# A state-space stage whose next batch's inputs are made between the scan's steps

## The reference, cut to what matters

```python
x = einsum('ed,bld->bel', in_proj_w, hidden_states)          # 256 -> 512 channels
u = silu(conv(x, conv_w, 4 taps) + conv_b)
dt_lo, Bm, Cm = split(einsum('ke,bel->bkl', x_proj_w, u))    # 16 + 16 + 16 rows
delta = softplus(dt_proj_w @ dt_lo + dt_proj_b)
state = state * exp(delta_t * A) + (delta_t * u_t) * B_t      # over the 512 positions
y_t = sum over states of state * C_t
y = (y + D * u) * silu(z)          # z: the normalized x; y is added to x
```

## Time and profile before

| | us |
|---|---|
| median of 3 runs (3116.88 to 3126.09) | 3119.8 |
| the profiled execution | 3117.0 |
| its span, first to last instruction | 3115.6 |
| VectorE busy over the span | 2025.2 (65%) |
| TensorE busy over the span | 2485.5 (80%) |

### The profile page before, as it was taken

How to read it: one execution, slowest core, us unless ns; L and a number is a source line. 1 busy time by engine, 2 the same in 40 slices (tenths; PEclk the granted TensorE clock), 3 DMA queues, 4 the chain that set the end, 5 groups by cost and what they waited for, 6 DMA issues and landing times. The chain is left out here.

```text
span 3115.6 us, 42764 instructions
## 1 busy us (share of the span) xinstructions
PE 2485.5 (80%) x11156; PEld 1737.0 (56%) x11174; DVE 2025.2 (65%) x3184; ACT 1250.8 (40%) x2245; POOL 1586.5 (51%) x1294
## 2 busy tenths in 40 slices
PE   7825655555979489999999983889989999999686
PEld 2301212214767367667777762677777777877443
DVE  3579999897868334554444446675776676565596
ACT  3424343443345232221121212545545545555365
POOL 2446565564047666666666626654664655444110
PEclk9869899898989799999999996999999999999899
DMA  2016666653369798887777745443443543342101
GB/s 84 9 41 214 219 210 223 219 202 118 141 238 339 264 316 287 306 277 247 247 235 255 248 148 180 145 139 126 146 140 105 166 139 115 95 136 82 54 0 54
DMA packets 260696, 538.30 MB, mean 173 GB/s; under 512 B 24401, under 2 KB 90065, under 8 KB 259809
## 3 DMA queue, kind: packets, MB, share of 16 engines
q1 hardware_dynamic: 207296, 347.98, 32.9%
q0 software_dynamic: 44032, 167.80, 16.3%
q10 hardware_dynamic: 9248, 21.11, 2.0%
HBM read 328.14 MB, written 208.67 MB: 172 GB/s over the span
## 5 line engine op out<-in xcount | busy, mean ns | idle before, releaser
L523 PE MATMUL ps_y<-c_state,ident 128*128 128x512 f32 x512 | 268.7, 651 | 205.5 <-DVE c_state L475 205.4
L448 POOL TENSOR_TENSOR b_u<-du,bc 128x1024 f32<-128x1024 f32 x128 | 301.3, 2354 | 214.5 <-DVE c_state L475 178.0
L1713 ACT ACTIVATE prob<-ps_s,neg,q_rs 128x512 f32<-128x512 f32 x256 | 197.1, 774 | 330.5 <-DVE neg L1893 330.5
L1230 PE MATMUL ps_o<-w_dn,hid_t 96*128 x632 | 308.4, 611 | 0.0
L1797 POOL TENSOR_SCALAR prob<-prob,rden 128x512 f32<-128x512 f32 x256 | 175.6, 696 | 253.9 <-DVE rden L1901 253.9
L523 PEld LDWEIGHTS ps_y<-c_state,ident 128*128 128x128 f32 x512 | 91.8, 198 | 381.8 <-DVE c_state L475 312.7
L467 DVE TENSOR_TENSOR_SCAN state<-ps_decay,b_u 128x1024 f32<-128x1024 f32 x128 | 293.1, 2290 | 16.1 <-issue 8.7
L1266 ACT ACTIVATE silu_g<-ps_gu 128x192 f32<-128x192 f32 x159 | 52.6, 331 | 546.5 <-PE ps_gu L1211 543.0
L419 ACT ACTIVATE ps_decay<-delta,a_neg 128x511 f32 x256 | 165.9, 681 | 225.5 <-DVE state L467 225.1
L1211 PE MATMUL ps_gu<-w_gu_high,rows_t_high 128*128 (+1 forms) x636 | 230.7, 363 | 11.0 <-POOL w_gu_low L1095 9.5
L1095 POOL TENSOR_TENSOR w_gu_low<-raw_gu,w_gu_high 128x1536 fp32r<-128x1536 f32 x64 | 222.4, 3475 | 12.0 <-POOL w_gu_high L1093 12.0
(11 more groups left out here) (317 smaller groups left out, 6071.5 us busy)
## 6 DMA issues: line engine op xcount, KB each, us to landing
rows_dram<-zeros SPq DMA_DIRECT2D x15, 3584.0 KB, 14.3
raw_gu<-in_gate_up POOLq DMA_DIRECT2D x64, 768.0 KB, 5.4
rows<-rows_dram SPq DMA_DIRECT2D x160, 256.0 KB, 3.9
y_dram<-y SPq DMA_DIRECT2D x158, 256.0 KB, 3.5
bc<-bc_dram SPq DMA_DIRECT2D x64, 512.0 KB, 5.8
w_q<-wq_dram SPq DMA_DIRECT2D x64, 512.0 KB, 3.7
w_o<-wo_dram SPq DMA_DIRECT2D x16, 2048.0 KB, 8.5
w_dn<-in_down POOLq DMA_DIRECT2D x64, 384.0 KB, 5.9
```

Of the source, the lines that this page charges most:

```text
L448: pool.tensor_tensor(out=b_u[:, ec % 2, :, :], in0=m.du[:, ds1(b * EC + ec), :].broadcast_to([P, G, SEQ]), in1=bc[:, par, 0, :, :], op=ALU ...
L523: mm = pe.matmul(ps_y[ec][:, :], c.ident[:, :], c_state[:, ec % 2, g, :], start=False, stop=False)
L1230: mm = pe.matmul(ps_o[par][:, :], hid_t[par][:, k, :], w_dn[:, ds1(slot), k, :].rearrange("p a f -> p (a f)"), start=k == 0, stop=k == 1)
L1713: act.activation(prob[:, qt, :], ps_s[qt % 2][:, :], ACT.Exp, scale=q_rs[:, k % 2, qt:qt + 1], bias=neg[:, qt:qt + 1], accum_out=den[:, qt ...
```

## The change

`ssm_inputs`, the first `norm_statistics` and `ssm_scan` become one function, `state_space`, without loops on the chip: all 128 steps are written out. Batch 0's inputs are made first, as before, with the statistics of the norm between. The inputs of batch b + 1 are made during the 32 steps of batch b: each engine, after its part of step q, runs `also(b, s)` with s = q % 32, which holds pieces of that work. The softplus becomes max(v, 0) + m + (log(1 + m) - ((1 + m) - 1)): `parts` makes Abs and Relu on ScalarE, `dens` and `rests` are one VectorE operation each for a block, and `both`, `sum_delta` and `delta_u` are one GpSimd operation each.

The steps of a batch now go through pairs of blocks: 16 steps over blocks 0 and 1, then 16 over blocks 2 and 3. Two banks hold the sums instead of four, and two others serve the inputs and the transposes. One load of B and C serves two steps, from a ring of three. Gates and additions to X are done block by block in `also`. The zero fills are spread over the 64 groups of two steps, some 4.6 tiles each.

```diff
-def ssm_inputs(nc, c, m, d):
+def state_space(nc, c, m, d):
...
+        STEPS = EC * NG
+        PAIR = 2 * NG
+        GROUPS = BATCH * STEPS // 2
+        BR = 3
...
+        def block_of(q):
+            b, s = q // STEPS, q % STEPS
+            return b, s, b * EC + s // PAIR * 2 + s % 2
...
+            def load_bc(g):
+                b, ng = g // (STEPS // 2), g % NG
+                wait(sp, product_made, 2 * (g - BR + 1))
+                for n in range(2):
+                    src = m.bc_dram[b:b + 1, n * DS + ng * G:n * DS + (ng + 1) * G, :]\
+                        .rearrange("a n l -> a (n l)").broadcast_to([P, G * SEQ])
+                    sp.dma_start(bc[:, g % BR, n, :, :].rearrange("p g l -> p (g l)"), src).then_inc(bc_loaded[g % BR], 16)
...
+            for g in range(GROUPS):
+                b, r = g // (STEPS // 2), g % (STEPS // 2)
+                if r == 0:
+                    sp.wait_ge(dbc_stored, (b + 1) * 16)
+                load_bc(g)
...
+                if r == 12 and b + 1 < BATCH:
+                    store_bc(b + 1)
+                for dram, skip, n in ((m.rows_dram, 0, FILLS * FILL), (m.y_dram, MINT, FILLS * FILL_Y)):
+                    first, last = g * n // GROUPS, (g + 1) * n // GROUPS
+                    if last > first:
+                        fill(dram, skip + first, skip + last)
+                        fills += 1
+            sp.wait_ge(filled, 16 * fills)
...
+            def convolve(ec, out):
+                for k in range(TAPS):
+                    mm = pe.matmul(out[:, :], conv_diag[:, ec * TAPS + k, :], x_pad[:, ec, k:k + SEQ],
+                                   start=k == 0, stop=k == TAPS - 1)
+                mm.then_inc(conv_done, 1)
...
+            def also(b, s):
...
+                if more and 4 <= s < 8:
+                    ec = s - 4
+                    if ec < 2 and b:
+                        pe.wait_ge(x_added, n - 1 + ec)
+                    if ec < 2 and not b:
+                        pe.wait_ge(pos_made, EC)
+                    if ec >= 2:
+                        pe.wait_ge(x_copied, nn + ec - 1)
+                    project(nb, ec, bank[ec % 2])
+                if more and s in (8, 9):
+                    ec = s - 8
+                    pe.wait_ge(x_copied, nn + 3 + ec)
+                    convolve(ec, bank[ec])
+                if more and s in (11, 12):
+                    ec = s - 9
+                    pe.wait_ge(u_made, nn + ec - 1)
+                    convolve(ec, bank[ec - 2])
+                if more and s == 14:
+                    project_u(nb, bank[0])
+                if more and s == 15:
+                    project_dt(nb, 0, bank[1])
+                if more and s == 16:
+                    project_dt(nb, 1, bank[0])
+                if s == 18:
+                    pe.wait_ge(*((pos_made, nn + 1) if more else (x_added, n)))
+                    turn(n, bank[1])
+                if s == 19:
+                    pe.wait_ge(*((pos_made, nn + 2) if more else (x_added, n - 1)))
+                    turn(n + 1, bank[0])
+                if more and s in (20, 21):
+                    pe.wait_ge(x_added, n + s - 19)
+                    project_dt(nb, s - 18, bank[(s - 19) % 2])
             pe.wait_ge(small_loaded, 128)
...
+            for q in range(BATCH * STEPS):
+                b, s, n = block_of(q)
+                e, r = s % 2, s % PAIR
+                if r == e:
+                    if n < 2:
...
+                        pe.wait_ge(y_gated, n - 1)
+                    pe.matmul(ps_y[e][:, :], d_diag[:, n % EC, :], slot(u, n), start=True, stop=False)
+                pe.wait_ge(product_made, q + 1)
+                for g in range(G):
+                    mm = pe.matmul(ps_y[e][:, :], c.ident[:, :], c_state[:, q % 2, g, :], start=False, stop=False)
+                mm.then_inc(product_used, 1)
+                if r >= PAIR - 2:
+                    pe.matmul(ps_y[e][:, 0:2], c.ident[:, :], zero2[:, :], start=False, stop=True).then_inc(y_summed, 1)
+                also(b, s)
...
+            def keep_x(b, ec, out):
+                act.wait_ge(x_made, b * EC + ec + 1)
+                wait(act, delta_made, (b - 1) * EC + ec + 1)
+                act.activation(x_pad[:, ec, TAPS - 1:], out[:, :], ACT.Copy).then_inc(x_copied, 1)
...
+            def parts(b, ec, out):
+                n = b * EC + ec
...
+                act.activation(mag[:, ec, :], out[:, :], ACT.Abs, bias=dt_b[:, ec:ec + 1]).then_inc(mag_made, 1)
+                act.activation(pos[:, ec, :], out[:, :], ACT.Relu, bias=dt_b[:, ec:ec + 1]).then_inc(pos_made, 1)
...
+            def decays(q):
+                b, s, n = block_of(q)
+                act.wait_ge(delta_made, n + 1)
+                wait(act, scanned, q - 1)
...
+            def also(b, s):
+                nb = b + 1
+                if s == 2:
+                    gates(b, (0, 1))
+                if s == 4:
...
+                    return
+                if 5 <= s < 9:
+                    keep_x(nb, s - 5, bank[(s - 5) % 2])
+                if s == 10:
+                    keep_u(nb, 0, bank[0])
+                    keep_u(nb, 1, bank[1])
+                if s == 13:
+                    keep_u(nb, 2, bank[0])
+                    keep_u(nb, 3, bank[1])
+                if s == 15:
+                    keep_dbc(nb, bank[0])
+                if s == 16:
+                    parts(nb, 0, bank[1])
+                if s == 17:
+                    parts(nb, 1, bank[0])
+                if s == 18:
+                    exponents(nb, (0, 1))
+                if s == 19:
+                    logarithms(nb, (0, 1))
+                if s == 21:
+                    parts(nb, 2, bank[1])
+                if s == 22:
+                    parts(nb, 3, bank[0])
+                if s == 23:
+                    exponents(nb, (2, 3))
+                if s == 24:
+                    logarithms(nb, (2, 3))
...
+            for q in range(BATCH * STEPS):
+                decays(q)
+                also(q // STEPS, q % STEPS)
...
+            def sum_delta(b, ec):
+                n = b * EC + ec
+                waits(both_made, n + 1)
+                waits(rest_made, n + 1)
+                waits(scanned, (b - 1) * STEPS)
+                pool.tensor_tensor(out=slot(delta, n), in0=pos[:, ec, :], in1=log_part(ec), op=ALU.add).then_inc(delta_made, 1)
...
+            def input_product(q):
+                b, s, n = block_of(q)
+                g = group_of(q)
+                waits(bc_loaded[g % BR], g // BR * 32 + 32)
+                waits(du_made, n + 1)
+                waits(scanned, q - 1)
+                waits(product_made, q - 2)
...
+            def also(b, s):
+                if b + 1 == BATCH:
+                    return
+                if s in (20, 21, 26, 27):
+                    both(b + 1, (20, 21, 26, 27).index(s))
+                if s in (22, 24, 28, 30):
+                    sum_delta(b + 1, (22, 24, 28, 30).index(s))
+                if s in (23, 25, 29, 31):
+                    delta_u(b + 1, (23, 25, 29, 31).index(s))
...
+            for q in range(BATCH * STEPS):
+                input_product(q)
+                also(q // STEPS, q % STEPS)
...
+            def rests(b, ecs):
+                for ec in ecs:
+                    n = b * EC + ec
+                    dve.wait_ge(den_made, n + 1)
+                    dve.wait_ge(log_made, n + 1)
+                    dve.tensor_tensor(out=log_part(ec), in0=log_part(ec), in1=den[:, ec, :], op=ALU.subtract)\
+                        .then_inc(rest_made, 1)
...
+            def apply_gate(n):
+                dve.wait_ge(y_summed, n + 1)
...
+            def also(b, s):
+                n = b * EC
+                if b and s == 0:
+                    apply_gate(n - 1)
+                if b and s == 3:
+                    add(n - 2, bank[0])
+                if b and s == 4:
+                    add(n - 1, bank[1])
+                if s == PAIR - 1:
+                    apply_gate(n)
+                if s == PAIR:
+                    apply_gate(n + 1)
+                if s == 19:
+                    add(n, bank[1])
+                if s == 20:
+                    add(n + 1, bank[0])
+                if s == STEPS - 1:
+                    apply_gate(n + 2)
+                if b + 1 == BATCH:
+                    return
+                if s == 19:
+                    dens(b + 1, (0, 1))
+                if s == 21:
+                    rests(b + 1, (0, 1))
+                if s == 24:
+                    dens(b + 1, (2, 3))
+                if s == 26:
+                    rests(b + 1, (2, 3))
...
+            dens(0, range(EC))
...
+            rests(0, range(EC))
+            scan(0)
+            for q in range(BATCH * STEPS):
+                if q + 1 < BATCH * STEPS:
+                    scan(q + 1)
+                product(q)
+                also(q // STEPS, q % STEPS)
+            last = BATCH * EC
```

(120 more changed lines are left out.)

402 lines of the change are left out of this document (134 added, 268 removed).

## The result

| | us |
|---|---|
| before, median of 4 | 3119.6 |
| after, median of 4 (3236.6 to 3262.2) | 3248.7 |
| ratio, 95% interval | 1.041 (1.036 to 1.046) |
| profiled execution of after, and its span | 3262.2, 3260.8 |

The kernel is slower by 129 us; 3271 was forecast, with a range of 3180 to 3336.

The account below looks back on a forecast made before the run. It took each 3.61 us step as bound by GpSimd's b_u and VectorE's product not running together. Terms 78.4 + 458.5 + 213 + 61 + 62 + 4 + 5.6 = 882.5, against 731.5, gave +151: 3271 us, range 3180 to 3336.

Parts of the forecast that it names:

- The mechanism: In eleven steps a batch ScalarE waits for TensorE, loses its lead, and the step becomes one chain.
- The start: Only batch 0's inputs come ahead of the scan, so the first product ends at 78.4 us.
- The waits and the clock: Three batches with pieces: chained steps add 213 us, TensorE at half clock behind gaps adds 61.
- plain steps: Scan steps without added waits: 3.61 us each, 127 after the first product, 458.5 us.
- the clock's share: TensorE passes behind gaps of waiting steps run at half clock: 61 us, bounds 0 and 124.
- Pieces of GpSimd and VectorE: Input pieces moved into the scan's steps: 62 us for three batches, 4 in the last; bounds 10 to 90.
- the pairs of `dens`: VectorE's differences within a batch's steps, put at 0.5 us.
- `rests` at s = 21: They feed GpSimd's sum_delta, holding b_u(23): about 4.3 us beside TensorE's chain, leaving GpSimd 1.2 behind.
- The tail: After the last product: sums, gate, transposes and two additions, 5.6 us.
- Late loads: Doubled loads of B and C during the scan, costed at nothing; bounds 0 and 32.3 us.
- The stages behind: Stages after the last addition to X, taken to be the same as before.
- u's steps: Waiting steps s = 10 and 13: 13.8 us each, 10.2 over a plain step, without the page's extra drain.

Follow-up runs that it names:

- e1: Changed kernel with ScalarE's pieces of the next batch's inputs three steps later: 3014.2 us, 0.965 of the kernel before.
- e3: Changed kernel plus six matmuls on zeros after each TensorE piece that ScalarE waits for, keeping TensorE at work: 3197.0 us, 1.026 of the kernel before.
- e2: Changed kernel with ScalarE's pieces one step later: 3074.6 us, 0.985 of the kernel before.
- e7: On top of e4, ScalarE's pieces two steps later than in the changed kernel, those of u three: 2989.6 us, 0.959 of the kernel before.
- e5: Changed kernel with ScalarE's pieces two steps later: 3017.1 us, 0.966 of the kernel before.
- e4: On top of e1, `dens` and `rests` made one a step and GpSimd's other pieces moved: 2992.5 us, 0.960 of the kernel before.
- e8: On top of e1, only the differences (`dens`) made one a step, GpSimd's pieces unmoved: 3005.5 us, 0.961 of the kernel before.
- e6: Changed kernel with TensorE's thirteen input pieces placed ahead of the sums of their step: 3095.5 us, 0.991 of the kernel before.

## Why the prediction was right

The mechanism, the sign and the place were right: see e1 and e3. By its terms, from the product ends in the profile after:

- **The start**: 75.5 for 78.4.
- **The waits and the clock**: 33 steps of 9.0 to 16.9 are 386.6 us, 267.5 over plain steps, for 213 + 61 = 274. With e3's clock the same steps are 344.8, so 225.6 over, for 213; the clock's share that e3 took away is 42, for 61.
- **Pieces of GpSimd and VectorE**: 846.5 - 75.5 - 458.5 - 267.5 = 45.0, for 66 (62 and the last batch's 4). This is the term that was mis-sized. A GpSimd piece costs 0.9 (steps of 4.5), not 1.52: while the product holds GpSimd off, the piece is already issued, and its wait and start fall in that time (the piece at 255.98 lasts 2.24 instead of 1.27, as the product ends at 257.10). Against it, the pairs of `dens` were put at 0.5, and the steps behind them are 3.6 over a plain one, 0.9 of it GpSimd's own piece. `rests` at s = 21 hold GpSimd's `sum_delta` as forecast; that lies beside TensorE's chain here and shows as a step of 9.2 once ScalarE's pieces are moved (e1).
- **The tail**: 851.6 - 846.5 = 5.1, for 5.6.
- **Late loads**: 7.0 us of GpSimd's waits, put at nothing. That holds only since the steps had grown: with plain steps they are 21.6 (e1), within the bound of 32.3.
- **The stages behind** were put at no change. The profile after has 2409 us there, before 2384; with the same code behind, the runs show 2385 (e3), 2388 (e2), 2390 (e7), 2394 (e5), 2395 (e4), 2396 (e1), 2398 (e8), 2409 (e6). The stage is 120 us longer, 31 less than forecast, and the 25 behind it made up for most of that in the profiled execution: that it took 3262 with 3268 forecast is in part luck. It was also the slowest of the four; the median, 3249, is 22 below the forecast. What makes those stages vary is open; no run was aimed at it.

The Trainium skill's "ScalarE: Activation LUTs", in "What ACT_TABLE_LOAD costs", gives another 1.38 us for a drain at each switch of table sets. The trace doesn't show it: with the clock held (e3), u's steps measured 13.8, as reckoned without, and there the load that starts at 343.13 lasts 1.28 and the Exp behind it starts at 344.43.

## What to carry to other kernels

Before putting work between the steps of a pipeline, write down for each engine how many steps it runs ahead or behind, and let a piece wait only for what an engine will have done by that time, not for what has a smaller step number. An engine that runs ahead and is made to wait for one that runs behind turns a step into the sum of all engines; here moving one engine's pieces by three steps turned a loss of 4% into a gain of 3.5%. Check every pair of engines: the worst step left after that, 9.2 us, was GpSimd made to wait for VectorE. Then count, for each pair that excludes each other, what the second piece in a step has to wait for.

## What the runs showed of the hardware

- Extra matmuls made the kernel faster: 0.43 us a pass against 0.86 at 1.2 GHz behind gaps of 5.3 us, 42 us over the stage.
- A VectorE operation with one input and 128x512 values is held off by GpSimd's operations like one with two: the 12 differences made beside the scan last 0.89 to 2.57 us, 1.87 in the mean, and with one in a step (e4) 0.41 to 1.49, 1.17 in the mean.
